# One loop of 78 expert slots in the first layer, with the shared expert's last products inside it

## The reference

```python
x = x + _L0_xattn_ref(ctx_1024, _layernorm(x), conv_w, conv_b, 512, 512, 4)
x = x + _L0_ffn_ref(_layernorm(x), ...)          # the part that is changed
x = x + _L1_xattn_ref(_layernorm(x), ctx_1024, ctx_1024, ...)
x = x + _L1_ffn_ref(_layernorm(x), ...)

def _L0_ffn_ref(X, ...):                          # E = 8 experts, K = 2 of them per row
    shared = silu(X @ sW1 + sb1) @ sW2 + sb2      # every row, 256 -> 128 -> 256
    activation = sqrt(softplus(X @ routing_W.T + expert_bias))
    top_vals, top_idx = top_k(activation, 2)
    y_e = silu(X @ rW1[e] + rb1[e]) @ rW2[e] + rb2[e]
    return shared + sum over the two chosen e of top_val * y_e
```

## Time and profile before

| | |
|---|---|
| timed runs, median | 827.2 us (826.39 to 827.79) |
| profiled execution | 822.08 us, span 820.2 us |
| PE busy over the span | 91% |
| mean DMA rate | 188 GB/s |
| first layer's slots 0 to 38 | 138 to 195 us |
| `shared(1)` | 195 to 207 us |
| first layer's slots 39 to 77 | 207 to 260 us |
| attention at its full pace | from 281 us |

### The profile page before, as it was taken

One profiled execution on the slowest core, in us unless ns is written; L12 is line 12 of the kernel. 1 busy time (PEld: TensorE's weight loads), 2 busy tenths in 40 slices (PEclk: granted clock), 3 DMA queues, 4 the chain that ended last, 5 costly groups with the idle time before them and its releaser, 6 DMA issues.

```text
span 820.2 us, 16199 instructions
## 1 busy us (share of the span) xinstructions
PE 749.1 (91%) x4633; PEld 653.7 (80%) x4633; DVE 530.4 (65%) x1423; ACT 489.3 (60%) x1379; POOL 429.7 (52%) x399
## 2 busy tenths in 40 slices
PE   4799987889898499999999999789999999999996
PEld 3546635676776399999998988689999999999995
DVE  5687857552665488888889888776543343365454
ACT  2337735555676488888877787356555454454541
POOL 3000655564687958888545778544652445333220
PEclk9899999999999799999999999899999999999998
DMA  8999997787899943663610444633444434565457
GB/s 248 343 285 308 332 300 257 241 276 227 184 268 241 320 121 81 163 153 70 210 63 2 161 163 148 206 104 120 140 137 142 144 104 133 179 210 177 161 178 233
DMA packets 128745, 154.47 MB, mean 188 GB/s; under 512 B 10875, under 2 KB 118550, under 8 KB 127638
## 3 DMA queue, kind: packets, MB, share of 16 engines
q1 hardware_dynamic: 102896, 112.55, 44.7%
q0 software_dynamic: 18624, 34.29, 15.8%
q10 hardware_dynamic: 7142, 6.59, 2.4%
HBM read 77.39 MB, written 76.00 MB: 187 GB/s over the span
## 4 chain that ended last, share of the span: by engine, by line
PE 70%; DVE 8%; issue 5%; ACT 5%; POOL 5%; DMA 4%; DVEq 1%; another core or an unknown queue 0%; SPq 0%; POOLq 0%; ACTq 0%
PE psum L849 24%; PE psum L1164 9%; PE psum L1142 8%; PE psum L1236 7%; PE psum L1241 6%; PE psum L1237 6%; POOL X L718 4%; PE psum L1152 3%; PE psum L1252 3%; ACT pr L1549 2%; PE psum L1215 2%; DMA X<-yl_dram,slots_y 1%; DMA yk_dram<-ys,L 1%; PE psum L1037 1%; PE psum L942 1%
## 5 line engine op out<-in xcount | busy, mean ns | idle before, releaser
L771 POOL DMA_INDIRECT yk_dram<-ys,L x52 | 53.6, 1031 | 136.2 <-ACT ys L1641 136.0
L718 POOL DMA_INDIRECT X<-yl_dram,slots_y x64 | 101.0, 1578 | 31.9 <-issue 14.2
L690 POOL DMA_INDIRECT xs_dram<-N,slots x64 | 65.9, 1029 | 97.0 <-DVEq L1943 58.4
L1549 ACT ACTIVATE pr<-psum,nmx 128x64 f32<-128x64 f32 x512 | 108.4, 365 | 6.8 <-DVE nmx L2314 6.6
L1236 PE MATMUL psum<-whi,xTh 128*128 x284 | 103.9, 366 | 3.4 <-ACT xTh L1603 2.4
L2410 DVE TENSOR_TENSOR hs<-psum,hs 128x384 f32<-128x384 f32 x71 | 39.7, 559 | 87.4 <-PE psum L1241 45.2
L1237 PE MATMUL psum<-wlo,xTh 128*128 x284 | 96.0, 338 | 0.0
L759 POOL DMA_INDIRECT xs_dram<-N,slots x64 | 69.7, 1090 | 35.9 <-ACT ys L1641 19.1
L1241 PE MATMUL psum<-whi,xTl 128*128 x284 | 74.1, 342 | 1.5 <-DVE xTl L2433 1.4
L751 POOL TENSOR_TENSOR pr<-pr,sm 128x1024 f32<-128x1024 f32 x32 | 62.2, 1944 | 19.5 <-DVE sm L2321 17.3
L1633 ACT ACTIVATE hs<-psum 128x384 f32<-128x384 f32 x71 | 34.9, 492 | 49.0 <-PE psum L1241 36.7
(11 more groups left out here) (370 smaller groups left out, 2041.2 us busy)
## 6 DMA issues: line engine op xcount, KB each, us to landing
fx<-xs_dram SPq DMA_DIRECT2D x78, 130.0 KB
yl_dram<-fy SPq DMA_DIRECT2D x78, 128.0 KB
xs_dram<-fill SPq DMA_DIRECT2D x4, 2340.0 KB, 14.1
xs<-xs_dram SPq DMA_DIRECT2D x71, 130.0 KB
wlo<-in_L_ffn_W_dram SPq DMA_DIRECT2D x4, 1536.0 KB, 11.4
xs_dram<-cz SPq DMA_DIRECT2D x1, 5070.0 KB, 24.2
xs_dram<-cz SPq DMA_DIRECT2D x7, 650.0 KB
X<-in_x_dram SPq DMA_DIRECT2D x4, 1024.0 KB, 11.7
```

Of the source, the lines that this page charges most:

```text
L690: po.indirect_dma_start(XS, bass.IndirectOffsetOnAxis(ap=slot[k][:, t:t + 1], axis=0), N0[:, t, :], None).then_inc(s[done], 16)
L718: po.indirect_dma_start(X[:, t, :], None, YL[b // 2], bass.IndirectOffsetOnAxis(ap=slot_y[k][:, t:t + 1], axis=0), compute_op=ALU.add).the ...
L771: po.indirect_dma_start(YK, bass.IndirectOffsetOnAxis(ap=yid[:, j:j + 1], axis=0), ys[j % YB], None).then_inc(s[f"y_out{j % YB}"], 16)
L1549: last = act(pr[b][:, S * h:S * h + S], bank[2 * b + h // 8][:, S * (h % 8):S * (h % 8) + S], ACT.Exp, bias=nmx[:, h:h + 1])
```

## The change

The two slot loops become one loop over 78 slots, so that PE, ACT, DVE and SP go from slot 38 to slot 39 as from any slot to the next; SP loads slot 39 when it is at slot 32, behind a wait for group 1's sends. All four ups and silus of group 1's shared expert come ahead of the loop (`hidden(q)` has four buffers now). Its downs are cut into 8 halves; half i sits at slot `HALVES[i]` = 9, 13, ..., 37, ahead of that slot's transposes, in PSUM bank 4. DVE's additions of the shared results are at slots 3, 9, 15, 21, 27, 30, 33, 40. `combined(1)` moves from slot 19 to slot 2 on DVE, `combine(1)` from slot 35 to slot 6 on PE. `SLOTS` is 4 instead of 5, so group 1's last send waits for slot 28 instead of about slot 34.

```diff
-BREAK, SLOTS = 4, 5
+BREAK, SLOTS = 4, 4
+HALVES = range(9, 38, 4)
+ADDS = (3, 9, 15, 21, 27, 30, 33, 40)
@@ SP
-                for j in range(first, first + AHEAD):
-                    load(j)
-                for j in range(first, last):
-                    if j + AHEAD < last:
-                        load(j + AHEAD)
+            def load_row(j):
+
+                if j % LS == 0:
+                    sent(j // LS)
...
+            for j in range(LA):
+                g, i = divmod(j, LS)
+                if j + AHEAD < LA:
+                    load_row(j + AHEAD)
+                sp.wait_ge(s["f_ys"], j + 1)
+                sp.dma_start(YL[g][i * P:i * P + P, :], fy[j % YB]).then_inc(s[f"ys_out{j % YB}"], 16)
+                if j == LS:
                     sp.dma_start(vraw, VD[0].rearrange("p (m c) n -> p m (c n)", c=2)).then_inc(s["v_in"], 16)
@@ PE
+            def shared_half(q, h, to):
+
+                for t in (2 * h, 2 * h + 1):
+                    o = to[:, D * (t % 2):D * (t % 2) + D]
                     mm(o, hidden(q)[:, t * P:t * P + P], sw2_sb[:, :], True, False)
                     last = mm(o, cT[:, q % LQ, :], b2w[:, t, :], False, True)
                     if t % 2:
                         last.then_inc(s["l_sy"], 1)
...
+                for j in range(LA):
+                    if j == 6:
                         combine(1)
-                    if j + 3 < last_:
+                    if j in HALVES:
+                        q, h = divmod(2 * LQ + HALVES.index(j), 2)
+                        if h == 0 and q == LQ:
+                            pe.wait_ge(s["pre_c_sb"], 7)
+                        pe.wait_ge(s["l_ev"], 2 * q + h)
+                        shared_half(q, h, bank[4])
+                    if j + 3 < LA:
                         xpose(j + 3)
...
-            for q in (LQ, LQ + 1):
+            for q in range(LQ, QUADS):
                 shared_up(q)
-            routed(0)
-            shared(1)
-            routed(1)
+            routed()
@@ ACT
+                    if j in HALVES:
+                        half_out(*divmod(2 * LQ + HALVES.index(j), 2), bank[4])
@@ DVE
-                    if j == LS // 2:
+                    if j == 2:
                         combined(1)
...
+                    if j in ADDS:
+                        shared_add(ADDS.index(j))
```

More of the change, by code:

```diff
@@ L459, in routed_rows @@
                 sp.wait_ge(s["l_sc2"], 16 * LT * (g + 1))
[L460 to L481 removed]
+            def load_row(j):
+                if j % LS == 0:
+                    sent(j // LS)
+                if j >= XB:
+                    sp.wait_ge(s["f_ys"], j - XB + 1)
+                sp.dma_start(fx[j % XB], XS[j * P:j * P + P, :]).then_inc(s[f"xs_in{j % XB}"], 16)
+            sp.wait_ge(s["vw_p"], 2 * PAIRS)
+            sp.wait_ge(s["a_p"], 2 * PAIRS)
+            for j in range(AHEAD):
+                load_row(j)
+            for j in range(LA):
[5 more added lines that the diff above has]
+                if j == LS:
+                    sp.dma_start(vraw, VD[0].rearrange("p (m c) n -> p m (c n)", c=2)).then_inc(s["v_in"], 16)
             def load(j, early=False):
@@ L1003, in shared_down @@
             def shared_down(q):
-                pe.wait_ge(s["pre_c_sb"], 6 + q // LQ)
+                pe.wait_ge(s["pre_c_sb"], 6)
                 pe.wait_ge(s["l_hs"], q + 1)
[L1007 to L1012, removed]
+                for h in range(2):
+                    if q:
+                        pe.wait_ge(s["l_ev"], 2 * q - 1 + h)
+                    shared_half(q, h, bank[(6, 5)[h]])
+            def shared_half(q, h, to):
+                for t in (2 * h, 2 * h + 1):
+                    o = to[:, D * (t % 2):D * (t % 2) + D]
                     mm(o, hidden(q)[:, t * P:t * P + P], sw2_sb[:, :], True, False)
@@ L1016, in shared_down, with routed @@
                         last.then_inc(s["l_sy"], 1)
[L1018 to L1028, removed]
+            def routed():
                 def xpose(j):
@@ L1033, in xpose @@
                         pe.wait_ge(s["f_xt"], j - 2)
-                    if j % 3 == 2 and j < first + 3:
-                        pe.wait_ge(s["l_ev"], 2 * LQ * (g + 1))
+                    if j == 2:
+                        pe.wait_ge(s["l_ev"], 2 * LQ)
                     for c in range(DC):
@@ L1433, in combined_turn @@
                 act(cT[:, :, :], bank[(7, 4)[g]].rearrange("p (q n) -> p q n", n=P), ACT.Copy).then_inc(s["pre_c_sb"], 1)
-            def shared(g):
-                q0 = LQ * g
-                for q in range(q0, q0 + LQ):
-                    if q0 + 2 <= q + 1 < q0 + LQ:
-                        silu(q + 1)
-                    shared_out(q)
             def split_high(k, m, v):
@@ L1462, in scale @@
                     act(fy[j % YB], bank[(7, 5)[j % 2]][:, 0:D], ACT.Copy, scale=fx[j % XB][:, D:D + 1]).then_inc(s["f_ys"], 1)
-                silu(first)
-                for j in range(first, last_):
-                    if j + 1 < last_:
+                silu(0)
+                for j in range(LA):
+                    if j + 1 < LA:
                         silu(j + 1)
                     scale(j)
-                    if j == LS - 4:
+                    if j == 6:
                         combined_turn(1)
-                    i = j - first - 4
-                    if g and i >= 0 and i % 4 == 0 and i < 32:
+                    if j in HALVES:
+                        half_out(*divmod(2 * LQ + HALVES.index(j), 2), bank[4])
+                    i = j - LS - 4
+                    if i >= 0 and i % 4 == 0 and i < 32:
                         if i == 0:
```

68 lines of the change are left out of this document (28 added, 40 removed).

## The result

| | before | after |
|---|---|---|
| timed, median | 827.5 us (4 runs, 826.39 to 828.26) | 834.09 us (3 runs, 832.38 to 837.6) |
| profiled execution, span | 822.08, 820.2 us | 834.09, 832.3 us |
| first transposes of the loop | 138.83 | 146.57 |
| POOL's first collect | 199.07 | 210.80 |
| attention at full pace | 281.09 | 292.39 |

The ratio is 1.0079 [1.004, 1.0118]. One run of 869.9 us at a granted clock of 0.84 was disturbed and is left out. The forecast was 835. In the two profiled executions the span grew by 12.1 us: the attention starts 11.3 us later, and behind it 0.8 us are added. As forecast, nearly everything was decided ahead of the attention.

What follows compares the result with a forecast made beforehand. POOL's chain from group 0's last store to the attention was taken as the bound. Terms 3.4 + 8.8 - 6.0 + 0.5 + 0.7 + 0.5 = +7.9 us gave 830 us profiled, 835 timed; range 829 to 841.5.

Steps and rivals of the forecast that it cites:

- Which chain: Group 0's last store, then POOL's 38 collects and scaling start the attention; the second slot loop is beside it, 5.9 us slack.
- Ups, +3.4: Ups of quads 6 and 7 ahead of the loop, where PE has no idle time to hide them: +3.4 us.
- Halves, +8.8, less 6.0 hidden: Eight halves in slots 9 to 37 add 8.8 us of PE time; 6.0 of 9.2 us of transfer stalls hide part.
- slot 38's place in the stream: PE has transposes of 41 and the up of 39 ahead of slot 38's down: +0.7 us.
- `combined(1)` had been put down as a loss: At slot 2 it holds DVE early: +1.1, less 0.6 for the stall it leaves at slot 19, +0.5 us.
- The store's landing, +0.5: Slot 38's store lands among loads of group 1, at least the 2.42 us of before: +0.5 us.
- SP's wait, 0: SP's wait for group 1's sends at slot 32 just passes: 0, at most some 2 us.
- vraw's load, put at 0: 1 MB load moved from ahead of slot 39's load to behind its store, needed 20 slots later: 0.
- T0: Landing of group 0's last store (slot 38), 198.17 us before; forecast to move by +7.9 us, to about 206.
- Behind T0, 0: POOL's 82.9 us from that landing to the attention stay as they are: 0, bounds -6 and +5 us.
- Relief of the DMA queues: Rival: spread shared work removes group 0's stalls and shortens POOL's landing waits: -3.4 us, 824 us; chance 0.15.
- Cold loop: Rival: PE idles at slot 61, its clock falls and slots 61 to 77 run slower: +21, 848 us; chance 0.05.

Runs made afterwards that it cites:

- all_spread: Changed kernel with the four ups at slots 39 to 45 and the halves at 47 to 61, every other slot, behind slot 38; ratio 1.0009.
- before_ups_late: Kernel before with the ups of quads 4 and 5 moved from ahead of the first loop to behind slot 38; ratio 0.999.
- ups_late_head2: Kernel before with two ups moved behind slot 38 and two of POOL's collects postponed into the attention; ratio 1.0035.
- all_late: Changed kernel with the four ups at slots 39 to 42 and the halves at 45 to 52, closely packed behind slot 38; ratio 1.0158.
- before_head2: Kernel before with HEAD = 2: 4 instead of 6 collects ahead of POOL's first scaling, the other two later in the attention; ratio 1.0017.
- before_slots4: Kernel before with SLOTS = 4 only, so group 1's sends are paced over slots 0 to 28 instead of 34; ratio 1.0022.
- before_again: Unchanged copy of the kernel before, run in a later series on another chip; one run, 830.4 us.
- after_again: Unchanged copy of the changed kernel, run in a later series on another chip; ratio to the kernel before 1.0081.
- double_before: Changed kernel with each half's four matmuls made twice in slots 9 to 37, ahead of slot 38; 827.17 us, ratio 1.0122.
- halves_late: Changed kernel with the eight halves moved from slots 9 to 37 to slots 39 to 53, behind slot 38; ratio 1.0024.
- late67: Changed kernel with the ups of quads 6 and 7 at slots 39 and 40 and the halves at 42 to 56; ratio 1.0072.
- double_after: Changed kernel with about as much extra PE work as eight halves, results unread, at slots 43 to 57; 819.77 us, ratio 1.0039.

## Why the prediction was right, step by step

- **Which chain.** Right in what starts the attention, not in the reading of the view. The prediction said that the chain does not run through the second slot loop; the view of before does run through it, from b0 k1's landing to 261.47. It is POOL's timeline that bears the prediction out: nothing but 0.30 to 0.31 us of issue stands ahead of the collects there, so the loop's side was close but not late. A - C stayed at 81.3 to 82.7 in nine of the twelve experiments. In three of the nine this is no proof: in all_spread, before_ups_late and ups_late_head2 the waits for landings were shorter (6.5, 6.7 and 6.3 us instead of 8.1) and POOL waited on the loop's side instead. Of the other three experiments, two touch what A - C is made of (all_late fills the room beside it, before_head2 takes collects out); before_slots4 had 84.0 with a first collect of 2.44 us. The removed joint gave nothing back: it went into the wait at slot 61, 3.0 us to 10.2 and 9.0.
- **Ups, +3.4.** They took 7.17 - 3.43 = 3.7 us, with no cover. Right.
- **Halves, +8.8, less 6.0 hidden.** From slot 9's down to slot 38's are 206.87 - 161.68 = 45.2 us. Less 29 x 1.10 and seven halves between (7.7) that leaves 5.6 us of stalls where about 3 were forecast; before it was 9.2. So 3.6 us were hidden there, not 6.0. The sum counts slot 38's place in the stream (+0.7) as a term of its own; with it 4.3 us were hidden, so the term was too large by 1.7 to 2.4. Its reason, that the stalls come from the transfers, is not shown either: of PE's 6.1 us of waits from 152 to 196 us in the trace of before, none is for a load, 3.4 are for ACT's `fh`, and the longest (1.66 at 192.79) stands behind a wait of ACT of 2.44 us for "remote". In the changed kernel's loop ACT has only 1.1 us of those instead of 3.5, so part of the 3.6 may be chance and not cover. The mis-sizing did not show, because slots 0 to 9 lost less than forecast: 161.68 - 146.57 = 15.1 us against 14.2 before, with a half and `combine(1)` in it (1.1 + 0.4), so about 0.5 us less for the rest, where `combined(1)` had been put down as a loss. Over slots 0 to 38 the loop grew by 60.3 - 55.7 = 4.6 us; the terms gave 8.8 - 6.0 + 0.5 + 0.7 = 4.0.
- **The store's landing, +0.5.** Wrong in sign, and small. The landing of slot 38's store is not in the rows of after; from its issue to the first collect are 210.80 - 208.02 = 2.8 us against 199.07 - 195.75 = 3.3 before. With the step from slot 38's down to its store this part is 0.6 us shorter.
- **SP's wait, 0.** The waits of SP's queue list 0.3 us for group 1's sends, once. Right. But vraw's load, put at 0, probably did cost: it was issued at 209.47 and took 7.6 us to land, and PE stood 3.83 us for the `fx` at 217.49 that was issued behind it. No run tests this. It lies behind T0, so slot 61's wait took it.
- **Behind T0, 0.** The two landing waits went from 8.09 to 7.88. Right; the bounds of -6 and +5 were far too wide. "Relief of the DMA queues" is out, since the DMA share stays at 0.85 to 1.02 from 206 to 292 us and the waits did not shrink. "Cold loop" is out too: the clock fell to 0.85 in the parked stretch, and POOL's scaling began at 290.40, 3.6 us after the loop's side had `sm` ready (286.52 + 0.25). That is 2.3 us less room than before, within what two executions of one kernel differ by (3.8 us in before_again, 5.4 in after_again).
- **The time.** The parts of the 8.1 us are: ups +3.7, slots 0 to 38 +4.6, from slot 38's down to the first collect -0.6, from there to the attention -0.4, behind it +0.8. The sum (830) stood for an undisturbed stretch ahead of the loop. The profiled execution was 834, of which 4.0 us are the two upstream differences. T0 came shortly before 210.8, not at 206, for the same reason. The timed ratio, over several runs, is 1.0079 and 1.0081, 6.6 us; the forecast was 835 / 827.2 = 1.0094, 7.9 us.
- **What was not foreseen** is that the hidden part is a property of the run as much as of the kernel. Added PE time of 8.8 us cost 4.8 us of C - L in double_before; removed, it gave 7.2 in halves_late and about nothing in late67. One term cannot hold for all of these. And double_after's 1.0039 leaves it open whether the change costs as much in sitting 1. That the total came out so near to 7.9 owes something to luck: 1.7 us too much taken as hidden, against 1.0 us too much put down for slots 0 to 9 and 1.1 for the store.

## What to carry to other kernels

Find the transfer that starts the longest serial stretch of another engine, and ask of every moved instruction on which side of it it lands; closing a gap behind it buys nothing if a later wait is for that engine. The chain of the profile names one path where two arrive together, so check it against the engine's own idle times. Work put into stalls is hidden in part only, and taking work out of a loop with stalls may give nothing: price both by an experiment that doubles it, ahead of that transfer and behind. If a free stretch is filled, spread the work over it, since one shared PSUM bank in neighbouring slots cost up to 1.1 us each time in all_late.

## What the runs showed that was not expected

- The same kernel had a median of 816.0 us (18 runs) in one sitting and 827.1 and 827.4 (19 and 35 runs) in the others. The first and the last of these are from the same chip, so it is not the chip. The traces put it ahead of the slot loop: with the same code, L was 136.3 and 137.2 in sitting 1 and 147.3 in after_again. From the first ups to the loop are 137.2 - 97.6 = 39.6 us in double_after and 147.3 - 97.8 = 49.5 in after_again. Most of these 9.9 us can be placed. In after_again ACT has three waits for "remote" in this stretch, 2.60, 2.31 and 3.46 us, and no trace of sitting 1 has one:

```profile
134.94 1.08 ACT L1427 ACTIVATE ysh<-psum 128x512 f32<-128x512 f32 x2 [3.46 <-remote]
```

PE stands 4.49 us for the last of them, until 135.68, the granted clock is 0.50 from 134 to 138, and the next two halves take 4.4 us, up to 140.08, instead of 2.2. What ACT waits for is open. The beginning of the stretch is slower too, at a DMA share near 1; busy times of double_after (sitting 1) and then of after_again (sitting 2):

```profile
90.00:110.00 20.00, 18.58 (x67) 9.88 (x66) 18.62 (x62) 13.25 (x23) 14.51 (x15) 1.00 1.02 321
```

```profile
90.00:110.00 20.00, 16.82 (x61) 9.56 (x60) 15.94 (x55) 12.49 (x21) 14.69 (x15) 1.00 1.02 321
```

- Between 30 and 50 us the granted clock averages 0.79 to 0.91 in eight of the fourteen traces, and the first ups start at 96.7 to 97.8 us; in the other six it averages 0.67 to 0.69, and they start at 100.1 to 100.7. Both happen to either kernel. The change does not touch this part, yet a single profile would charge it 2.9 us.
- A collect's cadence hardly depends on what else runs: 1.55 us and 0.30 of issue, with the loop beside it or without; of the 38 in a trace, a few take 1.6 to 2.5 us.
